# Finishing the gated output with one pass of ScalarE and a one-input pass of VectorE, with small sums moved to GpSimd

## The reference

```
x  = (x - mean_group) / sqrt(var_group + 1e-5)                    # gx
ch = conv1x1([mean_pixels(gx), max_pixels(gx)])                   # 16 numbers a group
channel_weight = sigmoid(norm(ch))                                # norm over one number: (ch - ch) * rsqrt(0 + eps)
pos_h, pos_w   = sigmoid(conv1x1(conv1x1(row and column means of gx)))
sx = conv3x3(gx * pos_h * pos_w) + b
spatial_weight = sigmoid(norm_over_pixels(sx) * w + b)
out = x_in + gx * channel_weight * spatial_weight
```

## Time and profile before

| | us |
|---|---|
| runs | 3528.66, 3526.47, 3527.98; median 3527.98 |
| profiled execution, its own time | 3526.81 |
| its span in the profile | 3524.7 |
| busy: DVE | 3421.2 |
| busy: PE | 3343.9 |
| busy: ACT | 2968.4 |
| busy: POOL | 1993.6 |

### The profile page before, as it was taken

How to read it: one execution, slowest core, us unless ns; L and a number is a source line. 1 busy time by engine, 2 the same in 40 slices (tenths; PEclk the granted TensorE clock), 3 DMA queues, 4 the chain that set the end, 5 groups by cost and what they waited for, 6 DMA issues and landing times.

```text
span 3524.7 us, 138640 instructions
## 1 busy us (share of the span) xinstructions
PE 3343.9 (95%) x52244; PEld 1601.2 (45%) x52244; DVE 3421.2 (97%) x1997; ACT 2968.4 (84%) x6274; POOL 1993.6 (57%) x907
## 2 busy tenths in 40 slices
PE   2999999999999999999999999999999999999996
PEld 1444444444444444444444444444444444444443
DVE  8899999999999999999999999999999999999995
ACT  2888888888888888888888888888888888888886
POOL 2566555655555565555566556556555655665562
PEclk9999999999999999999999999999999999999998
DMA  5466666666666667666666666666666666666654
GB/s 127 114 149 159 162 161 154 163 165 151 160 165 158 156 163 166 150 160 166 155 158 164 163 151 163 164 153 160 165 159 153 163 165 151 160 164 159 158 133 97
DMA packets 1115266, 547.03 MB, mean 155 GB/s; under 512 B 65712, under 2 KB 1114544, under 8 KB 1114544
## 3 DMA queue, kind: packets, MB, share of 16 engines
q1 hardware_dynamic: 836016, 403.05, 51.1%
q10 hardware_dynamic: 278528, 134.28, 13.8%
HBM read 268.63 MB, written 268.44 MB: 152 GB/s over the span
## 4 chain that ended last, share of the span: by engine, by line
DVE 33%; PE 29%; issue 22%; SPq 4%; ACT 3%; ACTq 3%; POOL 2%; DMA 2%; DVEq 0%; POOLq 0%
PE conv_ps L712 24%; DVE mx L624 8%; DVE sp_buf L579 7%; DVE sums L609 7%; DVE gated L664 4%; PE pos_ps L712 4%; SPq L240 4%; DVE fold L597 3%; ACTq L350 2%; DMA out<-sp_buf 2%; DVE sp_buf L589 2%; ACT sp_buf L361 2%; POOL rstd L301 1%; PE cw_ps L712 1%; POOL rstd L268 1%
## 5 line engine op out<-in xcount | busy, mean ns | idle before, releaser
L712 PE MATMUL conv_ps<-gated,W_conv 64*32 64x512 f32 x49152 | 2828.8, 593 | 56.4 <-ACT sp_buf L361 37.5
L712 PEld LDWEIGHTS conv_ps<-gated,W_conv 64*32 64x32 f32 x49152 | 1145.3, 106 | 1551.8 <-issue 1503.3
L287 POOL TENSOR_TENSOR gated<-gate_w,gate_hr 128x2048 f32<-128x2048 f32 x256 | 1175.1, 4590 | 20.2 <-POOL gate_hr L276 17.4
L361 ACT ACTIVATE sp_buf<-conv_ps,weights 128x512 f32<-128x512 f32 x1024 | 692.5, 677 | 207.5 <-DMA out<-sp_buf 120.4
L268 POOL TENSOR_TENSOR rstd<-var_e,consts 128x1 f32<-128x1 f32 x256 | 302.1, 1180 | 932.1 <-ACT var_e L398 932.1
L579 DVE SCALAR_TENSOR_TENSOR sp_buf<-xt,negm,sp_buf 128x2048 f32<-128x2048 f32 x256 | 600.3, 2345 | 30.1 <-ACT sp_buf L415 30.1
L589 DVE SCALAR_TENSOR_TENSOR sp_buf<-sp_buf,kfac,xt 128x2048 f32<-128x2048 f32 x256 | 602.1, 2352 | 9.0
L664 DVE SCALAR_TENSOR_TENSOR gated<-xt,negm,gated 128x2048 f32<-128x2048 f32 x256 | 591.2, 2351 | 14.2 <-POOL gated L287 14.2
L609 DVE TENSOR_REDUCE sums<-xt 128x32 f32<-128x4096 f32 x128 | 564.7, 4412 | 0.0
L624 DVE TENSOR_REDUCE mx<-xt 128x2 f32<-128x4096 f32 x128 | 564.3, 4408 | 0.0
L301 POOL TENSOR_TENSOR rstd<-var_e,consts 128x4 f32<-128x4 f32 x129 | 369.4, 2864 | 335.9 <-DVE var_e L651 335.9
(11 more groups left out here) (80 smaller groups left out, 1704.7 us busy)
## 6 DMA issues: line engine op xcount, KB each, us to landing
out<-sp_buf SPq DMA_DIRECT2D x2048, 128.0 KB, 2.5
xt<-in_x SPq DMA_DIRECT2D x1024, 128.0 KB, 3.4
xt<-in_x ACTq DMA_DIRECT2D x1024, 128.0 KB, 3.5
weights<-in_by_channel SPq DMA_DIRECT2D x1, 116.5 KB, 2.1
S_chan<-in_same_channel SPq DMA_DIRECT2D x1, 64.0 KB, 1.9
masks<-in_row_masks SPq DMA_DIRECT2D x1, 12.0 KB, 1.7
```

Source lines behind the costliest of these rows:

```text
L287: nc.gpsimd.tensor_tensor(gated[:, d, j, 1:1 + NB, 1:1 + W], gate_w[:, d, j].unsqueeze(1).to_broadcast([P, NB, W]), gate_hr[:, d, j].unsqu ...
L361: nc.scalar.activation(sp_buf[:, g, k * BB:(k + 1) * BB], conv_ps[:, k], ACT.Identity, bias=V["b_s3"], accum_out=sums2).then_inc(evac, 1)
L712: return nc.tensor.matmul(ps, lhsT, rhs, start=start, stop=stop)
```

## The change

1. The finish is written as (x - m)(1 + k s) + m. ACT gets `gate_plus_one` after each Sigmoid: `sp_buf = kfac * sp_buf + 1`, in place, over 2048 elements. `gate_x` then gives (x - m)(1 + k s), waiting on `one_plus`, and `add_x` is replaced by `add_mean`, a `tensor_scalar` that subtracts negm.
2. A third halving of the columns, `fold4` to `fold2` (512 elements), is done by POOL ahead of the first `rstd2_power`; PE's `positions` has two matmuls over it in place of four.
3. Of the channel norm ACT keeps the two scaled copies out of PSUM (`channel_in`, moved ahead of the first spatial gate) and the Sigmoid; subtraction, square and epsilon go to POOL (`channel_variance`, between the two `rstd2_power`), and the scaling too (`channel_norm`, first in POOL's body).
4. ACT's `evacuate(b, 7)` comes before `gates(a)`.

The core of the diff (new semaphores, their allocation and the counts of the weights' memsets are left out):

```diff
+            def fold_columns(u):
+                pool.wait_ge(fold4_done, u + 1)
+                if later(u, 1):
+                    pool.wait_ge(pos_mm, u)
+                nc.gpsimd.tensor_tensor(fold2[:], fold4[:, :, 0:2], fold4[:, :, 2:4], ALU.add).then_inc(fold2_done, 1)
+            def channel_variance(u, s):
+                pool.wait_ge(ch_in, 2 * u + 2)
...
+                nc.gpsimd.tensor_tensor(ch[:, 1], ch[:, 0], ch[:, 0], ALU.subtract).then_inc(ch_var, 1)
+                pool.wait_ge(ch_var, 3 * u + 1)
+                nc.gpsimd.tensor_tensor(ch[:, 2], ch[:, 1], ch[:, 1], ALU.mult).then_inc(ch_var, 1)
+                pool.wait_ge(ch_var, 3 * u + 2)
...
+                nc.gpsimd.tensor_tensor(var_e[:, (s + 1) % 2, 2:4], ch[:, 2], consts[:, 4:6],
+                                        ALU.add).then_inc(ch_var, 1)
+            def channel_norm(u, s):
+                pool.wait_ge(rstd_done, u + 2)
...
+                nc.gpsimd.tensor_tensor(ch[:, 3], ch[:, 1], rstd[:, (s + 1) % XS, 2:4], ALU.mult).then_inc(ch_norm, 1)
...
+            def gate_plus_one(u, s, j):
+                flat = sp_buf[:, 2 * (s % 2) + j].rearrange("p b w -> p (b w)")
+                act.wait_ge(sig2, 2 * u + j + 1)
+                act.wait_ge(kfac_done, u + 1)
+                nc.scalar.activation(flat, flat, ACT.Identity, scale=kfac[:, s, j:j + 1],
+                                     bias=consts[:, 8:9]).then_inc(one_plus, 1)
...
-                dve.wait_ge(sig2, n + 1)
+                dve.wait_ge(one_plus, n + 1)
...
-            def add_x(u, s, j):
...
-                dve.wait_ge(kfac_done, u + 1)
-                nc.vector.scalar_tensor_tensor(flat, flat, kfac[:, s, j:j + 1],
-                                               xt[:, s, j].rearrange("p b w -> p (b w)"),
-                                               ALU.mult, ALU.add).then_inc(final, 1)
+            def add_mean(u, s, j):
...
+                dve.wait_ge(fin_a, 2 * u + j + 1)
+                nc.vector.tensor_scalar(flat, flat, negm[:, s, j:j + 1], None, ALU.subtract).then_inc(final, 1)
...
-                    dve.wait_ge(pos_mm, u)
+                    dve.wait_ge(fold2_done, u)
...
-                        pe.wait_ge(fold4_done, c + 1)
+                        pe.wait_ge(fold2_done, c + 1)
...
-                        for i in range(4):
-                            mm(pos[:, :, NB:NB + W], W_cols[:, :], fold4[:, :, i], start=i == 0, stop=False)
+                        for i in range(2):
+                            mm(pos[:, :, NB:NB + W], W_cols[:, :], fold2[:, :, i], start=i == 0, stop=False)
```

More of the change, by code:

```diff
@@ L77, in conv_attention @@
         fold4 = sb("fold4", [P, 2, 4, W])
+        fold2 = sb("fold2", [P, 2, 2, W])
         W_rows_m = sb("W_rows_m", [P, P])
@@ L152, in conv_attention @@
         ch_mm = sem("ch_mm")
+        ch_in = sem("ch_in")
         ch_var = sem("ch_var")
@@ L314, in body @@
                 c, sc = t + 2, (q + 2) % XS
+                if real(t):
+                    channel_norm(t, q)
                 if real(a):
@@ L321, in body @@
                     gate_products(a, sa, 1)
+                if real(c):
+                    fold_columns(c)
                 if real(b):
                     rstd2_power(b, sb_, 0)
+                if real(a):
+                    channel_variance(a, sa)
                 if real(b):
@@ L441, in gates, with channel_in @@
                                          scale=rstd[:, s, j:j + 1], bias=b_pos[:, 1:2]).then_inc(gates_done, 1)
-            def channel_variance(u, s):
+            def channel_in(u, s):
                 act.wait_ge(ch_mm, u + 1)
                 if later(u, 1):
-                    act.wait_ge(cgate_done, u)
+                    act.wait_ge(ch_var, 3 * u)
                 for j in range(2):
                     nc.scalar.activation(ch[:, 0, j:j + 1], cw_ps[:, j:j + 1], ACT.Identity,
[L450 to L459, removed]
-                nc.scalar.activation(var_e[:, (s + 1) % 2, 2:4], ch[:, 2], ACT.Identity,
-                                     bias=consts[:, 4:5]).then_inc(ch_var, 1)
-            def channel_gate(u, s):
-                act.wait_ge(rstd_done, u + 2)
-                for j in range(2):
-                    nc.scalar.activation(ch[:, 3, j:j + 1], ch[:, 1, j:j + 1], ACT.Copy,
-                                         scale=rstd[:, (s + 1) % XS, 2 + j:3 + j]).then_inc(ch_norm, 1)
-                act.wait_ge(ch_norm, 2 * u + 2)
+                                         scale=rstd[:, s, j:j + 1], bias=V["b_cc"]).then_inc(ch_in, 1)
+            def channel_gate(u, s):
+                act.wait_ge(ch_norm, u + 1)
                 if later(u, 2):
@@ L480, in body @@
                 come = first_group(v) if real(v) else None
+                if real(b):
+                    evacuate(b, sb_, 7)
                 if real(a):
                     gates(a, sa)
-                if real(b):
-                    evacuate(b, sb_, 7)
                 if real(t):
@@ L502, in body @@
                     evacuate(t, q, 2)
+                if real(a):
+                    channel_in(a, sa)
                 if real(b):
                     spatial_gate(b, sb_, 0)
+                    gate_plus_one(b, sb_, 0)
                 load(v, vs, come, (3, 7))
@@ L508, in body @@
                     evacuate(t, q, 4)
-                if real(a):
-                    channel_variance(a, sa)
                 if real(t):
@@ L683, in body @@
                     gate_x(b, sb_, 0)
-                    add_x(b, sb_, 0)
+                    add_mean(b, sb_, 0)
                 if real(c):
@@ L691, in body @@
                     gate_x(b, sb_, 1)
-                    add_x(b, sb_, 1)
+                    add_mean(b, sb_, 1)
             turns(dve, body)
```

24 lines of the change are left out of this document (16 added, 8 removed).

## The result

The changed kernel takes **3892.38 us** (median of 4 runs, 3878.32 to 3897.86) against 3527.22 us (3525.45 to 3528.66) of the kernel before on the same chip: ratio **1.1029**, 95% interval 1.0998 to 1.1061. It is slower, as forecast, but by 365 us where 111 were forecast, and far outside the range. The profiled span is 3896.1 us, PE's mean granted clock 0.929 where it was 0.989.

A forecast was written before the change was run, and what follows sets the result against it. DVE bound the kernel at 26.69 us a unit, and the bound would move to ACT. Added to 3526.8 us, +86 for the units, +20 for loop turns and +5 for the ends gave 3638 us, range 3500 to 3740.

The forecast's parts named there:

- DVE's new operation: DVE's finish: a `tensor_scalar` over 2048 elements takes 1.15 us; upper bound 2.35, the operation it replaces.
- The bound moves to ACT: Each unit: the bound goes from DVE to ACT, which alone needs 26.53 us, each of two plus-ones adding 2.13.
- `add_mean` holds POOL up: POOL's chain after the gates: DVE's `add_mean` delays it by 0.8 us, bounds 0 and 0.8.
- `fold2`: POOL, ahead of its first power: 512 elements take 1.05 us, far end 2.1.
- The wait at L446: ACT at its first scale: waits for POOL's power 0.85 us in every unit.
- The unit without a turn: Unit away from the loop's jump back: ACT's 26.53 plus a wait of 0.85, 27.38 us, 0.69 more than 26.69.
- the sum without its turns: Whole kernel: +86 us over 125 full units and +5 for the ends.
- the term for the loop turns: 20 loop turns: PE stands 2.2 us; what exceeds its spare time is 0 to 2 us, say 1: +20 us.
- 1.3 + 0.8 us of spare time: Loop turns: PE has 1.3 us to spare before eviction 7, plus 0.8 in which POOL is held anyway.
- the missed gap: Rival, 12%: POOL's power comes after DVE began `modulate` and waits 2.35 us; 3680 us in some units, 3950 in all.
- PE's clock: Rival, 8%: granted clock halves after PE's stands before small matmuls, eviction 7 comes 1.8 us later; 3660 to 3740 us.

The follow-up runs named there:

- the unrolled kernel: The changed kernel with the loops written out on all five engines, no loop anywhere: 3610.09 us, ratio 1.0242.
- unrolled to unrolled: Both kernels without loops on any engine: the kernel before 3515.33 us (ratio 0.9970), the changed kernel 3610.09 us (ratio 1.0242).
- the shift: The changed kernel with 16 one-column matmuls more on PE ahead of everything, its loop head 64 instructions later: 3784.6 us, ratio 1.0753.
- the shifted kernel before: The kernel before with 48 one-column matmuls more on PE ahead of everything, its loop head 192 instructions later: 3586.64 us, ratio 1.0167.

## Why the prediction was right and wrong

- **DVE's new operation**: 1.15 us forecast, 1.29 measured, and 1.20 until the next one starts (1824.66 to 1825.86). The double rate is there for a column as scalar too.
- **The bound moves to ACT**: right. A plus-one adds 2.13 us, as forecast: at 1838.19 it takes 2.09 us, with 0.04 between the Sigmoid's end and its start.
- **`add_mean` holds POOL up**: right, and by 0.94 us, just over the 0.8 that the prediction had as its upper bound. The 32-element product takes 1.18 us while `add_mean` runs, and 0.24 at 1860.24, where DVE ran a one-input reduction. The Trainium skill's rule (SBUF — State Buffer, "SBUF: two separate sides") that a two-port mode locks the pair agrees with these two rows.
- **`fold2`**: 1.05 us forecast, 1.28 measured wherever nothing held it up. The straight line between two products of broadcasts was too low. By the Trainium skill's rate (GPSIMD Engine Reference, "3.1 Elementwise — side-by-side cycle accounting"), 2.6 cycles an element at 1.2 GHz, 512 elements are an estimated 1.11 us, and 1.28 with the 0.17 us by which the 0.24 us of 32 elements exceeds it. The trace agrees with that, but not for the product of two broadcasts: 2048 elements are 4.4 us by the rate and 3.61 in the trace.
- **The wait at L446**: 0.85 us forecast; 1.23 in this unit, 0.97 on the mean of the unrolled kernel (98.1 us in 101 waits). Of the 0.38 us that are over, `fold2` explains 0.23 and the longer hold-up 0.14.
- **The unit without a turn**: 27.38 forecast, 27.48 with loops, 27.3 without. The wait was larger than forecast, ACT's own work smaller (27.48 - 1.23 = 26.25 for 26.53): two errors of 0.3 us that cancel. From unrolled to unrolled the change costs 95 us; the sum without its turns was 86 + 5 = 91.
- **The step that failed** is the term for the loop turns, "What exceeds it is 0 to 2 us a turn, say 1: **+20**". Two of its assumptions were wrong, and one part it left out. First, it took PE's stand at a turn, 2.2 us, as a property of the loop that the change keeps. It depends on the position of the loop head, and removing two matmuls from PE's body moved that: 5.8 to 6.7 us. This is worth 108 us by the shift. Secondly, it let 1.3 + 0.8 us of spare time swallow most of a stall. Against 5.8 us that is little, and what exceeds it, eviction 7 passes on to the gates that the change queued behind it. POOL's chain then meets `modulate`, and ACT's 7.71 us become a unit 11.2 longer. With the shorter stall the loops still cost 3784.6 - 3610.1 = 174 us, 8 us a jump beside the 24 us of the common units. Thirdly, with no turn on PE at all 128 us are left, some 6 us a jump beside the same 24; the sum had no term for the turns of the other engines. ACT stands at its own, but no run shows how the 128 us share out. The loop has 19 turns, and the profile shows 19 branches with 18 jumps back, not 20. So against the +20 for the turns stand 282 - 10 = 272 us, and that is the whole miss: the rest of the sum, 91 us, came out as 95.
- **The rivals**: "the missed gap" was put at 12% as a matter of all or many units. It came at each of the 18 jumps and in eight other units of 31.1 to 31.4 us, seven of them right behind a turn, by the mechanism described: in these 26 POOL's first power takes 2.6 us. "PE's clock" seems to have a share at the turns, which no run separates: PE's stand of 2.63 us before its small matmuls was followed by a granted clock of 0.50, the lower of the two levels (1.2 GHz), and the 48 matmuls ahead of the turn, which began at it, took 3.87 us, where the same 48 took 2.81 in the shifted kernel before. In the common unit shown above eviction 7 does not wait for PE at all.

Its rows, from PE's timeline and from the windows (stretch, us, busy (x) of PE PEld DVE ACT POOL, PEclk, DMA, GB/s):

```profile
1841.18 0.37 PE L742 MATMUL gn_ps<-late_in,M_chan 128*128 128x21 f32 x2 [2.63 <-ACT sp_buf L400]
```

```profile
1845.00:1846.00 1.00, 1.00 (x24) 0.37 (x16) 1.00 (x1) 0.93 (x3) 1.00 (x1) 0.50 0.50 94
```

## What to carry to other kernels

Where a hand-written order runs in a loop on every engine, price its turns apart from the steady unit: take the units with a turn out of the row sums' starts and ask what absorbs the stall there. That cover is gone as soon as the bound moves to a chain between two engines, and an instruction put behind the last eviction inherits every delay of TensorE. Two runs tell the parts from each other: the same kernel without loops, and the same kernel with a few idle instructions ahead of the loop. And where an engine with 16% idle time takes over work of a full one, half of the work may fit where all of it does not: with `fold2` late one group by ACT's pass brought the unit from 26.7 to 25.6 us, both only to 26.2.

## What the runs showed that I had not expected

**A second stall behind the loop head, decided by its position.** The branch at the end of PE's body lasts the same in both kernels. The changed kernel's, then the one before's (times, duration in ns as least, median, greatest, and the first and last start in us):

```profile
L181 PEldq COMPARE_BRANCH  x19: 76/3938/4372, 405.8 to 3641.4; - x19
```

```profile
L177 PEldq COMPARE_BRANCH  x19: 76/3887/3992, 394.8 to 3286.7; - x19
```

Some 3.9 us, partly hidden by matmuls already issued. What differs is behind it, at the third or fourth instruction of the turn: PE stands 5.8 to 6.7 us instead of 2.2 to 2.9. 64 more instructions ahead of the loop took that away in the one kernel, 192 more brought it into the other. The Trainium skill (Runtime: NRT & Kernel Launch, "Instruction fetch mechanics") says that code is fetched in blocks of 256 instructions and that a taken branch out of the window forces a fetch. Both shifts fit such blocks, and in the two kernels with the long stall it lies one instruction apart. That the head then lies close to the end of one and a second fetch follows at once is my inference; the runs show the dependence on position and its price.

**Turns of engines other than PE.** The branch rows of ACT, DVE and POOL last 0.05 us, yet with PE unrolled ACT stands 44.3 us in 19 places, up to 3.2 us, and its kernel is 128 us above the one without any loop, 24 of them in the common units. Which share is ACT's alone was not tried.

**A wait that costs only in a loop.** With loops ACT stands 0.17 us at each square for its own small read (36.8 us in 214 waits), in the unrolled kernels that row is absent. Two of them a unit are enough for the difference between 27.48 and 27.3 us, though no run shows that they make it. The kernel before has them too, and hides them.

**A shared port hands the delay on.** Moving an instruction out of the way of `add_mean` gave the hold-up to the product behind it: 1.18 to 0.53 us for one, 3.61 to 4.62 for the other.
